# First pair of a fused adapter and MLP kernel: w1's last low parts on GpSimd, and another order of low parts and sums in steps 3 and 4

## The reference, cut to what matters

```python
# adapter, weights picked by language_ids
h = relu(x @ w1[lang] + b1[lang])                 # 512 -> 128
a = h @ w2[lang] + b2[lang]                       # 128 -> 512
y = x + a
x = x + layernorm(y) * gamma[lang] + beta[lang]
# MLP
h = gelu(x @ W1 + b1)                             # 512 -> 2048
shared = h @ W2 + b2                              # 2048 -> 384
expert = h @ We[expert] + be[expert]              # 2048 -> 128
x = x + concat(shared, expert)
```

## Time and profile before

| What | Value |
|---|---|
| median of 3 runs | 1429.12 us |
| lowest and highest run | 1428.09 and 1430.31 us |
| the profiled execution's own time | 1427.37 us |
| its span, from first to last instruction | 1425.5 us |
| granted TensorE clock | 1.0 throughout |
| TensorE busy | 1415.2 us (99%) |
| DVE busy | 1011.3 us (71%) |
| ScalarE busy | 522.9 us (37%) |
| GpSimd busy | 653.1 us (46%) |

### The profile page before, as it was taken

How to read it: one execution, slowest core, us unless ns; L and a number is a source line. 1 busy time by engine, 2 the same in 40 slices (tenths; PEclk the granted TensorE clock), 3 DMA queues, 4 the chain that set the end, 5 groups by cost and what they waited for, 6 DMA issues and landing times.

```text
span 1425.5 us, 18906 instructions
## 1 busy us (share of the span) xinstructions
PE 1415.2 (99%) x6220; PEld 1163.0 (82%) x6220; DVE 1011.3 (71%) x1645; ACT 522.9 (37%) x842; POOL 653.1 (46%) x644
## 2 busy tenths in 40 slices
PE   9999999999999999999999999999999999999999
PEld 6877878888888888888888888888888888888887
DVE  6999895776857867668677676767767687654434
ACT  4743444223442325332253323433234322432231
POOL 5987375451563514734157332564325633351101
PEclk9999999999999999999999999999999999999999
DMA  8646898457865677566774667746787457654332
GB/s 277 248 146 215 223 346 282 160 175 183 279 229 173 177 199 275 198 200 182 204 281 171 211 170 242 255 152 206 199 252 258 148 180 207 202 204 163 133 111 89
DMA packets 273957, 292.39 MB, mean 205 GB/s; under 512 B 129602, under 2 KB 230722, under 8 KB 265796
## 3 DMA queue, kind: packets, MB, share of 16 engines
q1 hardware_dynamic: 264068, 188.15, 43.9%
q10 hardware_dynamic: 9792, 103.03, 19.1%
HBM read 238.70 MB, written 52.43 MB: 204 GB/s over the span
## 4 chain that ended last, share of the span: by engine, by line
PE 89%; POOL 5%; DVE 3%; issue 2%; ACT 1%; SPq 0%; DMA 0%; DVEq 0%; ACTq 0%; POOLq 0%
PE down L275 15%; PE down L277 15%; PE down L276 15%; PE up_b L276 5%; PE up_b L275 5%; PE up_b L277 5%; PE up_c L275 4%; PE up_c L276 4%; PE up_c L277 4%; PE up_a L276 4%; PE up_a L277 4%; PE up_a L275 4%; POOL resid L1344 1%; PE aux L277 1%; PE aux L276 1%
## 5 line engine op out<-in xcount | busy, mean ns | idle before, releaser
L275 PE MATMUL down<-w,g 128*128 128x512 f32 x1024 | 399.0, 390 | 1.4 <-issue 0.6
L276 PE MATMUL down<-w,g 128*128 128x512 f32 x1024 | 398.7, 389 | 0.0
L277 PE MATMUL down<-w,g 128*128 128x512 f32 x1024 | 398.6, 389 | 0.0
L1361 POOL CAST w<-w_raw 128x256 fp32r<-128x256 f32 x125 | 70.6, 565 | 521.1 <-DMA w_raw<-m_we 521.1
L880 DVE TENSOR_TENSOR g<-g_raw,g 128x512 fp32r<-128x512 f32 x256 | 232.9, 931 | 80.0 <-ACT g L661 80.0
L275 PEld LDWEIGHTS down<-w,g 128*128 128x128 f32 x1024 | 192.3, 188 | 42.7 <-issue 1.7
L276 PEld LDWEIGHTS down<-w,g 128*128 128x128 f32 x1024 | 192.4, 188 | 39.7
L277 PEld LDWEIGHTS down<-w,g 128*128 128x128 f32 x1024 | 192.2, 188 | 39.8
L875 DVE TENSOR_TENSOR g_raw<-up_b,s 128x512 f32<-128x512 f32 x63 | 43.5, 691 | 183.0 <-PE up_b L277 170.0
L661 ACT CAST g<-g_raw 128x512 fp32r<-128x512 f32 x256 | 159.0, 622 | 8.0
L653 ACT ACTIVATE g_raw<-up_a,m_b_sb 128x512 f32<-128x512 f32 x64 | 44.1, 689 | 318.6 <-PE up_a L277 318.6
(11 more groups left out here) (225 smaller groups left out, 2506.7 us busy)
## 6 DMA issues: line engine op xcount, KB each, us to landing
w<-w_kept ACTq DMA_DIRECT2D x55, 1792.0 KB, 7.5
w<-w_kept SPq DMA_DIRECT2D x56, 768.0 KB, 5.0
w_raw<-m_we SPq DMA_DIRECT2D x128, 128.0 KB, 4.6
out<-resid SPq DMA_DIRECT2D x64, 256.0 KB, 4.4
xTs_raw<-xT SPq DMA_DIRECT2D x56, 256.0 KB, 3.0
xs<-x SPq DMA_DIRECT2D x56, 256.0 KB, 7.0
w_kept<-w SPq DMA_DIRECT2D x8, 1792.0 KB, 8.0
x_turned<-turned SPq DMA_DIRECT2D x112, 128.0 KB, 3.3
```

The source lines that it names most:

```text
L275: eng.matmul(bank, a_hi, b_hi, start=opens, stop=False, skip_group_check=True)
L276: eng.matmul(bank, a_hi, b_lo, start=False, stop=False, skip_group_check=True)
L277: return eng.matmul(bank, a_lo, b_hi, start=False, stop=closes, skip_group_check=True)
L1361: eng.tensor_copy(hi, values).then_inc(pool_eh[b], 1)
```

## The change

It has four parts, all in the first pair.

1. DVE, step 3: the low part of C12 leaves its place ahead of u2 and goes to the end of the step. w2's low part goes ahead of c22. The moments of tile 3 leave the end of the step.
2. DVE, step 4: the moments of tile 3 come right after q. The low part of C22 (of step 3) leaves its place ahead of u2 and goes behind the adapter's additions. GpSimd, step 4: the low part of the adapter's weights goes between the two pairs of bias additions.
3. Step 7: the 1024 columns of w1's low part move from DVE to GpSimd, behind its 768. Product 5 of the second pair's step 0 and the store wait for GpSimd's semaphore instead.
4. ScalarE, step 7: w1's high part goes ahead of C11's gelu and cast.

```diff
 pe_p5
         if i is pairs[1] and k == 0:
-            eng.wait_ge(dve_w1, GROUPS)
+            eng.wait_ge(pool_w1, 4)
 act_step
+        if i is first and k == GROUPS - 1:
+            act_w1_hi(eng, k + 1)
         act_g(eng, i, k, C11)
-        if i is first:
+        if i is first and k < GROUPS - 1:
             act_w1_hi(eng, k + 1)
-    def dve_rest_w1_lo(eng):
-
-        eng.wait_ge(act_w1hi, GROUPS)
-        eng.tensor_tensor(w1[:, 0, LO, A22:7, :], w1_raw[:, 0, LO, A22:7, :], raw(w1[:, 0, HI, A22:7, :]),
-                          ALU.subtract).then_inc(dve_w1, 1)
 dve_first_step
         dve_sum_q(eng, i, k)
+        if k == 4:
+            dve_moments(eng, m, 0, 3)
...
-        if k > 2:
+        if k > 3:
             dve_g_lo(eng, i, k - 1, C12)
-        if k > 3:
+        if k > 4:
             dve_g_lo(eng, i, k - 1, C22)
...
-        dve_sum_c22(eng, i, k)
         if k == 3:
             dve_w2_lo(eng, k - 1)
-        if k == GROUPS - 1:
-            dve_rest_w1_lo(eng)
+        dve_sum_c22(eng, i, k)
...
         if k == 2:
             dve_g_lo(eng, i, k - 1, C12)
+            dve_g_lo(eng, i, k - 1, C22)
+        if k == 4:
             dve_g_lo(eng, i, k - 1, C22)
...
             dve_sum_c21(eng, i, k)
+            if k == 3:
+                dve_g_lo(eng, i, k - 1, C12)
+                return
 pool_first_w1_lo
-            s = slice(A11, A22)
+            s = slice(A11, A22) if n == 2 else slice(A22, S3 + 1)
 pool_first_step
         if k == 4:
             pool_biases(eng, m, 1, 0)
+            eng.wait_ge(aw_split, m.front(4, 3))
+            pool_aw_lo(eng, m, 1, 1)
             pool_biases(eng, m, 1, 1)
...
-        if k == 4:
-            eng.wait_ge(aw_split, m.front(4, 3))
-            pool_aw_lo(eng, m, 1, 1)
         pool_weight_sums(eng, k + 1)
         if k == GROUPS - 1:
             pool_first_w1_lo(eng, 2)
+            pool_first_w1_lo(eng, 3)
 keep_w1
-        eng.wait_ge(dve_w1, k)
         if k == GROUPS:
-            eng.wait_ge(pool_w1, 3)
+            eng.wait_ge(pool_w1, 4)
+        else:
+            eng.wait_ge(dve_w1, k)
```

## The result

| What | Before | Changed |
|---|---|---|
| median of 20 runs each, beside each other | 1427.9 us | 1430.34 us |
| lowest and highest | 1426.37, 1430.31 us | 1429.22, 1431.93 us |
| the profiled execution's own time, span | 1427.37, 1425.5 us | 1430.40, 1428.6 us |
| ratio, 95% interval | | 1.0018 [1.0011, 1.0024] |

A forecast was written before the change was run, and what follows sets the result against it. TensorE, busy 99% of the span, was taken as the bound. A 0.6 us lag from step 5 less 0.1 us gained at the boundary gave +0.5 us on 1429.12, put at 1429.5 us, range 1427.6 to 1431.1.

The forecast's parts named there:

- Step 3: In step 3, TensorE's waits for u2 and w2's low part go, leaving it 1.56 us early at step 4.
- C21 takes the lead: In step 4, the second `pe_down` half waits for C21's low part, shrinking the 1.56 us lead to under 0.5.
- u2 and c12 of step 4: In step 4, u2 comes near 118.8, the sliver closes, and TensorE passes c12 0.6 us earlier.
- The late root, the sums, w1's low part, c12 of step 5: Steps 4 to 5: moved moments delay these in turn; the 0.6 us lead becomes a 0.6 lag, at worst 1.3.
- the 0.5 us of less sharing: In step 4, GpSimd's work up to the sums' end was to shrink 0.5 us, with less beside DVE's low parts.
- Handed on, not grown: In step 6, DVE's 1.34 us wait for TensorE ahead of u2 lets the 0.6 us lag pass on without growing.
- The boundary: Between the pairs, moving 1024 columns to GpSimd gains 0.1 us, bounds 0.2 lost and 0.5 gained.
- the cover of 2.83 us: At the boundary, the later wait for B22 hides up to 2.83 us of `pe_down` lateness; beyond it TensorE pays.
- the forecast's own last sign: Second pair: product 3's last matmul starting over 1 us from 208.99 would show the forecast's sum wrong.
- Rival 1: Steps 4 to 5: early GpSimd sums let the lead survive, with 0.5 at the boundary: -0.8 us, 1428.3; chance 0.20.
- rival 2: Steps 3 and 4: every wait closes and the boundary shifts in full: -3.3 us or more, 1425.8; chance 0.03.
- rival 3: Boundary: GpSimd's longer chain ends beyond the cover, losing 1.2 us: 1430.9 with the lag; chance 0.15.

The follow-up runs named there:

- e3: The change with tile 3's moments back at the end of step 3 and C12's low part of step 2 behind q; 1427.96 us, ratio 1.0001.
- e5: The change with tile 3's moments back at the end of step 3, C12's low part behind q, and step 7 as before; 1428.58 us, ratio 1.0004.
- e9: The change plus four GpSimd beta additions of sample 1 put behind the sums of steps 4 and 5; 1430.15 us, ratio 1.0015.
- e1: The kernel before with only the change's edits of steps 3 and 4, step 7 as before; 1430.17 us, ratio 1.0019.
- e6: The kernel before with another DVE order in steps 3 to 5, fewer low parts ahead of u2, old boundary; 1428.44 us, ratio 1.0006.
- e8: The old-boundary kernel with fewer low parts ahead of u2, plus four beta additions behind the sums of steps 4 and 5; 1430.05 us, ratio 1.0017.
- e10: The kernel before with only four GpSimd beta additions put behind the sums of steps 4 and 5; 1427.27 us, ratio 0.9998.
- e4: The change plus 14 unread transposes of 128 columns ahead of the boundary's second half-layer; 1429.30 us, ratio 1.0012.
- e11: The kernel before with reordered steps 3 to 5, late beta additions, 1024 columns on GpSimd, ScalarE's old order and 14 transposes; 1428.99 us, ratio 1.0008.
- e2: The kernel before with only the change's step 7 edits on GpSimd and ScalarE; 1428.08 us, ratio 1.0002.
- e7: The kernel before with only the 1024 columns moved to GpSimd in step 7, ScalarE's order as before; 1427.72 us, ratio 0.9998.
- e12: The kernel before with only tile 3's moments moved from the end of step 3 to behind q of step 4; 1429.35 us, ratio 1.0012.

## Why the prediction held, and where its size was off

The forecast of no difference beyond 0.2% and the range held, but it gave +0.5 us and the change costs +2.4. That 1429.5 came so close to 1430.34 (0.84 us) was luck: it started from a median of three runs that lies 1.2 us above that of twenty. By its steps, all with the 0.72 taken off:

- **Step 3: right.** 1.56 us of lead forecast, 1.67 measured, both waits gone.
- **C21 takes the lead: right, a little more than forecast.** The half of `pe_down` starts at 112.90, forecast 112.2 to 112.6. The sums of step 3 end 0.5 us later than before, where I had them up to 0.3 earlier.
- **u2 and c12 of step 4: right in kind.** u2 at 119.03 (118.8 forecast), the sliver gone; TensorE passes c12 0.21 us earlier, 0.6 forecast.
- **The late root, the sums, w1's low part, c12 of step 5: the mechanism right, its size the failed term.** The sums end at 128.29, forecast 127.1 and 127.7 at worst. The root ends at 115.5, 0.3 to 0.6 us later than I had it (q is 0.3 late), and GpSimd needs 12.8 us from there to the end of the sums, before 12.6: the 0.5 us of less sharing wasn't there. By being late, the sums slid beside DVE's low part and finishes (L882, L980): three of them took 1.18 or 1.19 us that had taken 0.74 before, one 0.73 that had taken 1.17, and that offset what the biases gained. The Trainium skill (SBUF — State Buffer, "Who interferes with whom") names the lock-out; the trace agrees that an addition costs more beside DVE. The question left out was beside what the moved work now lands. So w1's low part starts at 130.05 and not 128.8, TensorE waits 0.40 for it where I saw none, and c12 ends at 147.0, forecast 145.8. Lag 2.10 instead of 0.6, beyond my bound of 1.3. e3 and e5 show that it hangs on the moved moments, e9 that 1.34 us of it went through the sums.
- **DVE's own queue: left out of the forecast.** It is done with what stands ahead of w1's low part at 128.8, 1.5 us later than before: C22's low part is new there (0.83 us), and the low part and finishes ahead of it took 0.9 us more. So even with the sums in time (e9) w1's low part starts at 128.7, where before it was 127.29.
- **Handed on, not grown: right.** 2.10 at steps 6 and 7 and at the second pair.
- **The boundary: right at full clock, the clock not foreseen.** With the lag off too, `pe_down` starts at 199.3 (199.3 to 199.8 forecast), and the cover of 2.83 us absorbs it. Both low parts took 4.67 us on GpSimd, forecast 4.32. I had overlooked that product 5 needs T1's low parts, behind the 1024 columns; its 1.18 us only take part of the same wait. What a boundary costs is best counted from the landing of w1's raw columns. The old boundary hands its lateness on one for one (e1, e6, e8, e10); the new one, where the clock stayed up, hands on 0.3 us less (0.47 late at the landing and 0.13 behind product 7 in e3, 2.29 and 1.97 in e4, 1.66 and 1.32 in e11). Forecast was a gain of 0.1, bounds 0.2 lost and 0.5 gained. With the clock down it loses: 1.96 becomes 2.48 in the change, -0.10 becomes 0.41 in e2, 0.09 becomes 0.58 in e7. So the halved clock cost 0.82 to 0.85 us there, more than the 0.3 us gained. By the forecast's own last sign the sum fails: with 0.72 off, the last matmul of product 3 starts near 212.4 and not within 1 us of 208.99, by the lag of 2.1 and that clock.

Rival 1 fails (no lead is left at step 5), rival 2 with it, and rival 3 too: GpSimd does not pass the cover. The Trainium skill (GPSIMD Engine Reference, "4.1 Engine selection") says that two-input elementwise work is about twice as slow there. The trace agrees: 4.67 us for 1792 columns against DVE's 2.03. It did not decide, since the cover was there.

## What to carry to other kernels

Before a small operation is moved, ask which other engine's queue stands behind it: here 1.67 us of DVE's moments held GpSimd's root, and through it work that TensorE needed some 30 us later. The engine's own queue is to be added up as well: whichever of the two comes last sets the start. A stretch of work that shifts in time also changes what it shares memory with, so its duration is to be taken from what runs beside its new place. And a lead won ahead of a place that another chain times (here GpSimd's, from a transfer) ends at that place, so lateness there is to be counted from the transfer's landing.

## What the runs showed of the hardware

TensorE's clock fell to half (1.2 GHz) for eight to eleven matmuls behind the waits at the boundary, in some executions of a kernel and not in others: full clock in 23 of 33 executions of before (one series), 3 of 20 of the change and none of 11 of e9. In before, executions at mean clock 1.0 took 1427.39 us on average, those at 0.998 took 1428.70. Held against the landing of w1's raw columns it cost, by an estimate, 0.82 to 0.85 us in the profiled executions of the change, e2 and e7. In e5 and e12 the profiled execution shows it behind the last wait of the old boundary (0.55 and 0.62 in the window 212 to 215 us), where it cost 0.6 us, so it isn't the new order alone. What decides it in one execution and not the next stays open.
